# Moving one chunk's shared expert to the end of a routed mixture-of-experts block, with a wait inside the scatters and a rearranged start

## What is computed

```python
x = layernorm(x + attention(x))            # 8 heads, 2 key/value heads, window 32
shared = (silu(x @ sw1) * (x @ sw2)) @ sw3 # hidden width 256
probs = softmax(x @ rw + rb); w, idx = top_k(probs, 2); w = w / sum(w)
routed = sum over the two experts e of w_e * ((silu(x @ ew1[e]) * (x @ ew2[e])) @ ew3[e])
x = layernorm(x + shared + routed)
```

## Time and profile before

| | us |
|---|---|
| median of 3 runs | 234.68 |
| lowest, highest | 229.27, 235.91 |
| the profiled execution | 228.97 |
| its span, first to last instruction | 227.2 |

### The profile page before, as it was taken

One profiled execution on the slowest core, in us unless ns is written; L12 is line 12 of the kernel. 1 busy time (PEld: TensorE's weight loads), 2 busy tenths in 40 slices (PEclk: granted clock), 3 DMA queues, 4 the chain that ended last, 5 costly groups with the idle time before them and its releaser, 6 DMA issues.

```text
span 227.2 us, 3459 instructions
## 1 busy us (share of the span) xinstructions
PE 171.9 (76%) x974; PEld 119.0 (52%) x974; DVE 111.8 (49%) x360; ACT 107.8 (47%) x229; POOL 98.6 (43%) x110
## 2 busy tenths in 40 slices
PE   7499598698686657699678999999999899960000
PEld 2096577677574534456345656566666465650000
DVE  7875498589659929658123112121221221894070
ACT  2578968867945521312023555565556455650000
POOL 8440001006722766635700156465565544688330
PEclk9969999999999996999799999999999999996555
DMA  5995000000110111426530022333322036003310
GB/s 114 356 437 228 3 1 1 3 0 12 54 32 0 40 54 35 117 62 139 134 82 0 3 69 61 110 94 84 77 61 70 12 103 210 15 21 115 109 57 23
DMA packets 19458, 18.17 MB, mean 80 GB/s; under 512 B 3027, under 2 KB 17754, under 8 KB 19312
## 3 DMA queue, kind: packets, MB, share of 16 engines
q1 hardware_dynamic: 16432, 13.28, 20.2%
q0 software_dynamic: 2496, 4.24, 5.9%
q10 hardware_dynamic: 512, 0.45, 0.6%
HBM read 11.47 MB, written 7.39 MB: 83 GB/s over the span
## 4 chain that ended last, share of the span: by engine, by line
PE 47%; DVE 15%; issue 12%; POOL 7%; ACT 6%; DMA 5%; another core or an unknown queue 4%; ACTq 1%; POOLq 0%; DVEq 0%; SPq 0%
PE gu L574 18%; PE att L472 5%; POOL z_rows L1202 5%; PE q_bank L612 4%; PE att L586 3%; PE att L612 3%; PE att L566 3%; DMA bias<-biases 3%; PE q_bank L597 3%; PE att L552 2%; PE att L488 2%; ACT qT L706 2%; DVE mx L884 2%; DVE x L933 2%
## 5 line engine op out<-in xcount | busy, mean ns | idle before, releaser
L1202 POOL DMA_INDIRECT z_rows<-y,xin x46 | 45.6, 992 | 48.2 <-ACT y L790 36.6
L574 PE MATMUL gu<-w,xt 128*128 x92 | 45.7, 617 | 4.1 <-DVE h L1037 1.2
L1040 DVE TENSOR_TENSOR h<-sil,gu 128x512 f32<-128x512 f32 (+1 forms) x24 | 15.9, 663 | 61.8 <-ACT sil L776 57.1
L1194 POOL DMA_INDIRECT x_list<-x,pos x32 | 31.4, 981 | 16.5 <-issue 8.5
L776 ACT ACTIVATE sil<-gu 128x512 f32<-128x512 f32 (+1 forms) x24 | 13.9, 579 | 29.1 <-PE gu L574 26.8
L574 PEld LDWEIGHTS gu<-w,xt 128*128 128x128 f32 x92 | 15.5, 189 | 19.9 <-issue 19.9
L472 PE MATMUL att<-kM,qT 96*128 96x128 f32 x128 | 17.6, 297 | 8.2 <-ACT kM L719 3.6
L472 PEld LDWEIGHTS att<-kM,qT 96*128 96x128 f32 x128 | 16.4, 209 | 9.7 <-issue 9.7
L488 PE MATMUL att<-vbd,probT 128*128 128x128 f32 x128 | 17.1, 282 | 4.2 <-ACT probT L751 2.9
L1166 POOL TENSOR_TENSOR vareps<-mv,eps 128x4 f32<-128x4 f32 x4 | 0.8, 200 | 44.6 <-DVE mv L926 44.6
L488 PEld LDWEIGHTS att<-vbd,probT 128*128 128x128 f32 x128 | 15.3, 191 | 6.0 <-issue 3.6
(11 more groups left out here) (116 smaller groups left out, 289.0 us busy)
## 6 DMA issues: line engine op xcount, KB each, us to landing
w<-weights SPq DMA_DIRECT2D x1, 3456.0 KB, 16.6
xin<-x_list SPq DMA_DIRECT2D x46, 65.0 KB
z<-z_rows SPq DMA_DIRECT2D x3, 512.0 KB
x_list<-blank SPq DMA_DIRECT2D x18, 65.0 KB, 2.4
out<-result SPq DMA_DIRECT2D x3, 256.0 KB, 2.3
z_rows<-y,xin POOLq DMA_INDIRECT x46
xT<-x_cols SPq DMA_DIRECT2D x2, 256.0 KB, 5.7
xr<-x_rows SPq DMA_DIRECT2D x2, 256.0 KB, 7.0
```

The costliest lines, as they stand in the source:

```text
L574: mm = pe.matmul(gu_half[q], xt[:, pair % 2, q * P:(q + 1) * P], w[:, bass.ds(at[first_tile(pair) + q], CT)], start=True, stop=True)
L1040: dve.tensor_tensor(blocks(h[:, i % RING, 0:n * HIDDEN], HIDDEN), blocks(sil[:, i % 2, 0:n * HIDDEN], HIDDEN), blocks(gu[:, 0:n * CT], CT) ...
L1194: pool.indirect_dma_start(x_list[PART_OF[n]][:, :], bass.IndirectOffsetOnAxis(ap=pos[:, n, k, j:j + 1], axis=0), x2[:, n * ROWT + j, k * R ...
L1202: pool.indirect_dma_start(z_rows[g][:, :], bass.IndirectOffsetOnAxis(ap=xin[:, r, q, R_ID:R_ID + 1].bitcast(U32), axis=0), y[:, r, q, :], ...
```

## The change

- The shared iterations of chunk 3 move from i = 6 and 7 to i = 30 and 31. Routed pairs start at i = 6. The two use other PSUM banks (`ends_banks`), and their sum lands in the bank of `turn_rows`. `add_shared(3)` moves behind the loop. Combining starts at i = 26 (was 29), `scale2` at 28; GpSimd's `rstd2_of` for pieces 0 to 2 follows the scatters of pairs 17, 18 and 19 (was 19, 20, 21). Some of chunk 3's routing steps come one iteration later.
- `make_table(0)` moves on VectorE from ahead of the loop to iteration 1, behind `norm1(3)`; `turn(3)` goes ahead of `read_ends(0)`. `rank(2)` goes ahead of `up_shared(0)`.
- TensorE reads the offsets of one pair at a time, ahead of that pair's `turn_rows`, in place of 31 and 15 values.
- In each `scatter(n)` GpSimd waits, ahead of the fifth DMA, until the chunk's first four have landed.
- The constants shrink (ones are set on the chip, the table's constants are loaded for one partition), their larger part goes on SyncE's queue behind the first chunk's rows, the table's part ahead of the weights. ScalarE's queue has the biases ahead of the first constants. The wait for the larger part moves behind the first chunk's shifts.
- Warm-up products 12 → 8; eight zero products (`FILL_IN`) between `project_kv(0)` and the first scores.

The core of the diff:

```diff
-SHARED_ITERS = 2 * CHUNKS
-R_AT = [SHARED_ITERS, SHARED_ITERS + PAIRS[0]]
-ITERS = R_AT[1] + PAIRS[1]
+FIRST_SHARED = 2 * (CHUNKS - 1)
+R_AT = [FIRST_SHARED, FIRST_SHARED + PAIRS[0]]
+R_END = R_AT[1] + PAIRS[1]
+ITERS = R_END + 2
...
-WARM_UP = 12
+WARM_UP = 8
+FILL_IN = 8
...
+        turns = [gu_half, [att[2][:, :], att[3][:, :]]]
+        ends_banks = [[post[:, :], att[3][:, :]], gu_half]
...
+        SUMS_AT = R_AT[1] + 4
...
             sp.dma_start(xr[:, 0:ROWT, :], rows[:, 0:ROWT, :]).then_inc(xrow_in[0], 16)
+            sp.dma_start(cst[:, C_TRI:C_CUTS], consts[:, C_TRI:C_CUTS]).then_inc(place_in, 16)
...
+            sp.dma_start(cst[0:1, C_CUTS:C_END], consts[0:1, C_CUTS:C_END]).then_inc(cuts_in, 16)
             sp.dma_start(w[:, :], weights).then_inc(weights_in, 16)
...
             project_q(0)
             project_kv(0)
+            for _ in range(FILL_IN):
+                pe.matmul(post[:, :], idle[:, 0:P], idle[:, :], start=True, stop=True)
...
+            rank(CHUNKS - 2)
             up_shared(0, 0, 0)
-            rank(CHUNKS - 2)
...
-                if i == R_AT[0] - 1:
-                    at = fetch_weights(0)
-                if i == R_AT[1] - 1:
-                    next_at = fetch_weights(1)
-                if i + 1 < ITERS and pair_of(i + 1) is not None:
+                if pair_of(i + 1) is not None:
+                    at[i + 1] = fetch_weights(pair_of(i + 1))
                     turn_rows(pair_of(i + 1))
+                if i == ITERS - 1:
+                    down_routed(pair_of(i - 2), at[i - 2])
...
-                if i == 2:
+                if i == 3:
                     transpose_x2(last)
-                if i == 3:
+                if i == 4:
                     route(last)
-                if i == 4:
+                if i == 5:
                     rank(last)
...
             act.dma_start(pattern[GD:MROWS, :], masks).then_inc(mask_in, 16)
+            act.dma_start(bias[:, :], biases).then_inc(const_in, 16)
             act.dma_start(cst[:, 0:C_TRI], consts[:, 0:C_TRI]).then_inc(const_in, 16)
-            act.dma_start(bias[:, :], biases).then_inc(const_in, 16)
-            act.dma_start(cst[:, C_TRI:C_END], consts[:, C_TRI:C_END]).then_inc(place_in, 16)
...
+            turn(last)
             read_ends(0)
-            turn(last)
-            make_table(0)
             for i in range(ITERS):
                 hidden(i)
                 if i == 0:
                     norm1(last)
                 if i == 1:
+                    make_table(0)
+                if i == 2:
                     scale1(last)
-                if i == 3:
+                if i == 4:
                     logits(last)
-                if i == 4:
+                if i == 5:
                     gates(last)
                     places(last)
                     read_ends(1)
                     make_table(1)
-                for n in range(CHUNKS):
+                for n in range(CHUNKS - 1):
                     if i == 2 * n + 3:
                         add_shared(n)
-                if R_AT[1] + 5 <= i < R_AT[1] + 8:
-                    combine(i - R_AT[1] - 5)
-                if i == R_AT[1] + 7:
-                    scale2(0)
-            scale2(1)
-            scale2(2)
+                if SUMS_AT <= i < SUMS_AT + 3:
+                    combine(i - SUMS_AT)
+                if SUMS_AT + 2 <= i < SUMS_AT + 5:
+                    scale2(i - SUMS_AT - 2)
+            add_shared(last)
...
                 for j in range(first, last):
                     for k in range(2):
+                        if (j, k) == (2, 0):
+                            pool.wait_ge(scattered[PART_OF[n]], 16 * (2 * ROWT * PARTS[PART_OF[n]].index(n) + 4))
...
                 scatter_results(pair)
-                if PAIRS[0] + 3 <= pair < PAIRS[0] + 6:
-                    rstd2_of(pair - PAIRS[0] - 3)
+                piece = pair + FIRST_SHARED + 3 - SUMS_AT
+                if 0 <= piece < 3:
+                    rstd2_of(piece)
```

More of the change, by code:

```diff
@@ L72 @@
 C_ID = 0
[L73 to L79, removed]
+C_DEN = C_ID + P
+C_TRI = C_DEN + GROUPS
+C_BASE = C_TRI + P
+C_IOTA = C_BASE + 2 * EXPERTS
+C_PLACE = C_IOTA + EXPERTS
 C_NOWHERE = C_PLACE + 2 * CHUNKS * ROWT
-C_STEP = [C_NOWHERE + 1, C_NOWHERE + 1 + EXPERTS * STEPS[0]]
+C_BO = C_NOWHERE + 1
+C_CUTS = C_BO + D
+C_STEP = [C_CUTS, C_CUTS + EXPERTS * STEPS[0]]
 C_UPTO = C_STEP[1] + EXPERTS * STEPS[1]
@@ L536, in rank, with fetch_weights @@
                 mm.then_inc(rank_mm, 1)
-            def fetch_weights(g):
-                pe.wait_ge(table_done, g + 1)
+            def fetch_weights(pair):
+                g, t = part_of(pair), first_tile(pair)
+                if t == 0:
+                    pe.wait_ge(table_done, g + 1)
                 _, values = nc.values_load_multi_w_load_instructions(
-                    table[g][0:1, T_W:T_W + TILES[g]], engines=PE_ONLY, min_val=0, max_val=SHARED * WRAW,
+                    table[g][0:1, T_W + t:T_W + t + width(pair)], engines=PE_ONLY, min_val=0, max_val=SHARED * WRAW,
                     skip_runtime_bounds_check_because="an expert's number is a count of 8 comparisons")
@@ L565, in up_shared @@
                 for part in range(2):
-                    mm = pe.matmul(gu_shared[i % 2][part], w[:, at + part * HIDDEN:at + part * HIDDEN + P], x2T[:, tokens(n)],
+                    mm = pe.matmul(gu_shared(i)[part], w[:, at + part * HIDDEN:at + part * HIDDEN + P], x2T[:, tokens(n)],
                                    start=True, stop=True)
@@ L574, in up_routed @@
                     mm = pe.matmul(gu_half[q], xt[:, pair % 2, q * P:(q + 1) * P],
-                                   w[:, bass.ds(at[first_tile(pair) + q], CT)], start=True, stop=True)
+                                   w[:, bass.ds(at[q], CT)], start=True, stop=True)
                 mm.then_inc(up_mm, 1)
@@ L690, in _ @@
                     down_shared(i - 2, *shared_of(i - 2))
-                elif pair_of(i - 2) is not None:
-                    down_routed(pair_of(i - 2), at if i - 2 < R_AT[1] else next_at)
+                elif pair_of(i - 2) is not None and i < ITERS - 1:
+                    down_routed(pair_of(i - 2), at[i - 2])
         @block.scalar
@@ L763, in rows_turned @@
                 act.wait_ge(xt_mm, pair + 1)
-                after(act, up_mm, SHARED_ITERS + pair - 1 if pair >= 2 else 0)
+                after(act, up_mm, FIRST_SHARED + pair - 1 if pair >= 2 else 0)
                 n = width(pair) * P
@@ L780, in hidden_turned @@
                 act.wait_ge(ht_mm, pair + 1)
-                after(act, down_mm, SHARED_ITERS + pair - RING + 1 if pair >= RING else 0)
+                after(act, down_mm, FIRST_SHARED + pair - RING + 1 if pair >= RING else 0)
                 n = width(pair) * HIDDEN
@@ L835, in _ @@
             last = CHUNKS - 1
-            for i in range(ITERS + 3):
+            for i in range(ITERS):
                 if pair_of(i + 1) is not None:
@@ L1046, in add_shared @@
                 dve.wait_ge(down_mm, downs_of_shared(n))
-                dve.tensor_tensor(base[:, n * ROWT:(n + 1) * ROWT, :], blocks(q_bank[:, :], D),
+                dve.tensor_tensor(base[:, n * ROWT:(n + 1) * ROWT, :], blocks(shared_sums(n)[:, :], D),
                                   x2_k[:, n * ROWT:(n + 1) * ROWT, 0, 0:D], ALU.add).then_inc(base_done, 1)
@@ L1292 @@
         c[0, C_BASE + g * EXPERTS:C_BASE + (g + 1) * EXPERTS] = begin
-        c[:, C_STEP[g]:C_STEP[g] + EXPERTS * STEPS[g]] = (begin[:, None] + P * np.arange(STEPS[g])).reshape(-1)
+        c[0, C_STEP[g]:C_STEP[g] + EXPERTS * STEPS[g]] = (begin[:, None] + P * np.arange(STEPS[g])).reshape(-1)
     token = np.arange(CHUNKS * ROWT)[None, :, None] * P + row[:, None, None]
```

66 lines of the change are left out of this document (41 added, 25 removed).

## The result

The changed kernel took 219.94 us (median of 4 runs, 218.01 to 220.72) against 231.98 us before (median of 4, 228.25 to 235.91): 0.960 of the time, interval 0.948 to 0.973. The forecast was 220.5 in 213.5 to 228.5. The profiled execution has a span of 218.8 us, 8.4 under the 227.2 of before, where the sum had −10.6. The 220.5 was that sum, 218.4, with 2.1 added for the spread between runs. The total came out, most of its terms did not.

A forecast was written before the change was run, and what follows sets the result against it. The prediction saw no single limit, with the routed loop's work unchanged and gains on the road to the first pair. Terms −1.0 − 2.5 − 8.1 + 1.0 = −10.6 took 228.97 to 218.4; forecast 220.5 with spread, range 213.5 to 228.5.

The forecast's parts named there:

- Start: Chunk 0's scores: zero products fill 2.56 us of idleness before them; 1.0 us gained, bounds 1.6 gained, 0.8 lost.
- cold projections: First projections at half clock after eight warm-up products: loss about 0.8; as a rival, 1.8 worse, 220.2, chance 0.11.
- Hold at 64.36: VectorE's 3.65 us wait in chunk 2's attention goes; with a smaller one near 78, 2.5 us gained, bounds 0 and 3.65.
- The cause of the holds: TensorE completions seem held back in the second half of eight scatters in a row; their count inferred as cause.
- The rival that holds stay: Holds end with the issuing of scatters, not by count; gain only 4.5, time 224.5; chance 0.16.
- Last attention product to routed products: Stretch from last attention product to first routed product: 36.3 us becomes effectively 28.2; gain 8.1, bounds 4 and 11.
- Its roads: Three ways to the first routed product: GpSimd ready at 17.3, SyncE's loads at 17.9, TensorE's shared work done at 18.0.
- the landing hidden: New wait in each scatter call, +1.2 us on GpSimd; for chunk 2 it hides behind the rstd work.
- Base addition behind the second table: Second table on VectorE sits ahead of the second base addition, for which a shared down product waits: 1.1 us lost.
- Reading by pair: Routed loop: 24 offset loads of one or two values hide while TensorE's sequencer runs ahead; zero.
- loads exposed: Rival: each pair's offset load delays TensorE in the routed loop; at 1.2 us each, 29 lost and 247; chance 0.05.
- Tail: After the routed loop: moved shared iterations hidden, but GpSimd waits once for its rstd input; 1.0 us lost, bounds 0 and 3.

The follow-up runs named there:

- b_start: Kernel before with eight warm-up products in place of twelve and eight zero products ahead of the first scores, on the other chip; 224.67 us, 1.003 of before.
- a_eight: Changed kernel without the wait in mid-scatter, eight scatters in a row again, first chip; 227.62 us, 0.988 of before.
- a_again: Changed kernel once more, unedited, as yardstick of the first chip's job; 218.76 us, 0.954 of before.
- second execution: The unedited changed kernel run again on the first chip; attention 67.6 us, 218.76 us in all.
- b_wait4: Kernel before with one addition: GpSimd waits after four scatters of a chunk until they have landed, first chip; 228.38 us, 0.983 of before.
- b_nomove: Kernel before with the change's other edits, but shared iterations, constants and first table left in place, other chip; 222.84 us, 0.996 of before.
- a_ variants: Changed kernel on the other chip with old start, offsets read a part at once, or no wait in mid-scatter; 217.04, 216.89 and 217.38 us.
- a_again_2: Changed kernel unedited, as yardstick of a later job on the other chip; 217.39 us, 0.975 of before.
- c_order: Changed kernel with a chunk's first four scatters issued ahead of the next chunk's rstd, other chip; 222.06 us, 0.987 of before.
- c_warm: c_order with zero products (6, 4 and 4) added ahead of the scores of chunks 1 to 3, other chip; 215.77 us, 0.972 of before.
- b_gap: Kernel before with a fill of about 1 us on GpSimd in mid-scatter in place of a wait, first chip; 228.98 us, 0.996 of before.
- a_eight_2: Changed kernel without the wait in mid-scatter, repeated on the other chip; 217.38 us, 0.964 of before.

## Why the prediction came out, step by step

- **Total:** 220.5 forecast, 219.94 measured, by errors that cancel, which is luck. Profile against profile the sum was −10.6 and the measured −8.4: start and attention came out 5.85 worse than the sum, the way to the routed products 2.0 better, tail and loop 1.7 better. The 2.1 added for the spread happened to cover the rest.
- **Start, −1.0:** the mechanism was there (3.81 for 5.44 us), but by the runs the term is zero. Two steps failed. The loss by cold projections was weighed as the exception and came in five of ten profiles. And it was taken tacitly that the other half-clock stretches stay where they were; chunk 1's scores were slow in eight of those ten, as in three of the four profiles with the old start, though not in the one that the sum started from. How much each took back stays open.
- **Hold at 64.36, −2.5:** gone, as forecast. By stretches without other losses it was worth less: before took 68.1, which is 3.2 over b_start's 64.9; 1.6 of that is chunk 0's slow scores, so about 1.6 is the hold's. This is an estimate across two chips; on one chip, a_eight's attention is 1.5 over a_again's.
- **Start and hold together** were to bring 3.5 and lost 2.35 in the profiled execution: two half-clock stretches, together 6 us over b_start. In the second execution, with one stretch, attention took 0.5 less than before.
- **The cause of the holds:** that they go with long rows of scatters, and mostly last until these are issued, held on the chip that has holds; four in a row are nearly harmless there (1.05 to 1.33 us late, off the path). But the count alone is not the cause: the other chip issues twelve in a row without one. The rival that holds stay is refuted for VectorE's two waits; one hold of ScalarE's stayed at a place where it cost nothing.
- **Last attention product to routed products, −8.1:** measured −10.1. The table's steps would split it into 4.2 for the holds (41.1 to 36.9, b_wait4), 0.6 for reading by pair with rank first (36.3) and 5.3 for the move, but they cross chips, and 3.4 of the 4.2 are half-clock products that before had and b_wait4 had not. On the chip without holds the steps are 39.3 (b_start), 36.3 (b_nomove) and 29.6 to 31.7 (the changed kernel and its a_ variants): 3.0, and 4.6 to 6.7 for the move. The hold's own share is then some 1.8 (before against b_start, an estimate across chips).
- **Its roads,** t from the last attention product's end, 83.02: the table started at t = 6.5 (forecast 6.9), SyncE's loads at 19.0 (17.9). That was GpSimd's road, forecast 17.3: its first scatter of chunk 2 came 0.8 late, at 88.45, and from there to the loads it took 13.55, not 12.7, because of 0.85 us of waiting behind the rstd, where the prediction had the landing hidden (the profile says "issue" here, and names the landing at the same place in a_again_2 and c_order). The rows were there at 21.4 (forecast 21.3), as they landed 2.4 after the loads' start rather than 3.4. TensorE was done at 19.8, not 18.0, as the half-clock product came early, at 97.55. It waited 1.6, not 3.3, and the product behind the wait ran at full clock: 1.88, not 3.6. Hence 25.2 for the first routed product, not 27.1. The slow stretch of the clock was misplaced: it followed the wait for the norm (3.56 us), not that for the rows.
- **Base addition behind the second table, 1.1:** seen, 108.19 to 112.86 is 4.67 where the period is 3.58.
- **Reading by pair, zero:** right in the loop and, in the new order, at its head. The rival "loads exposed" is refuted (77.4 against 77.7).
- **Tail, +1.0:** wrong in sign and small; −0.4. GpSimd waited 2.15 us for its rstd input once, and that was made good in the slack of later pairs entirely, not mostly.

## What to carry to other kernels

A gain on an engine whose clock rises and falls can only be counted once one has seen where its next slow stretch falls; compare stretches between fixed points of several executions, not two spans. A long row of indirect scatters on one queue can hold back what other engines see of TensorE, on one of the two chips tried; with a break of 1.3 us after four the changed kernel takes nearly the same on both. And work moved to the end of a loop pays when it stood ahead of the loop's first data: here 5 to 6 us, about the 2 × (1.9 + 1.06) = 5.9 us that two shared iterations take, with nothing lost in the tail.

## What the runs showed of the hardware

- The holds (completions of TensorE taken up 1 to 4 us late while GpSimd issues a row of eight indirect scatters) were in all four profiles with such rows from one chip, beside those of before and after, and in none of six from the other. Their mechanism stays open; a break of 1 us in the issuing prevented VectorE's two, landing wasn't needed. Chip and job are not separated.
- Executions of the same kernel differ by one or more half-clock stretches (granted 0.50) of TensorE, each worth 1 to 3 us in the attention part; the same kernel had its stretch from 44 to 52 in one execution and not in the other.
- Ahead of the first rows, idle times of TensorE of 4.1 us were all three times followed by an up product of 3.4 to 3.6 us in place of 1.9 (a_eight, c_order and c_warm), those of 2.15 to 2.21 us three times out of four (before, b_start and b_gap; b_wait4 had 1.93), one of 1.9 us in part (a_again_2, 2.54), and those of 1.6 to 1.8 us never (after, a_again and a_eight_2, 1.88).
